# Two-layer decoder on one core: four engine blocks joined into one, with explicit waits at the stage borders

## The chip, the cores and the metric

The kernel runs on one core of a Trainium2 chip. The metric is the device time in microseconds (us) of the slowest core; with one core that is the time of the run. The engines of a core are PE (TensorE, matrix products), DVE (VectorE), ACT (ScalarE), POOL (GpSimd) and SP (SyncE, which here issues nearly all DMAs).

## The reference

The reference is a decoder of six steps, each added to the rows x (4 batches of 256 tokens, 256 wide) and followed by a layer norm:

```
x = _layernorm(x + _L0_attn_ref(x, ...))           # 16 heads of 128, causal, biases
x = _layernorm(x + _L0_xattn_ref(ctx_512, x, ...)) # top-76 graph of the context
x = _layernorm(x + _L0_ffn_ref(x, ...))            # 32 masked ternary experts, top-1
x = _layernorm(x + _L1_attn_ref(x, ...))           # 16 heads, 4 key heads, rotary
x = _layernorm(x + _L1_xattn_ref(x, ctx_512, ...)) # cross attention with a norm inside
x = _layernorm(x + _L1_ffn_ref(x, ...))            # 16 experts, top-4, and a shared one
```

Everything is float32; products are made as three products of high and low parts.

## The kernel before

The program has four stages, one after the other, each written as a function with a body for each of the five engines:

- `attention(c, 0, ...)`: the first attention, in 16 steps (`s`), one pair of heads for half the tokens each. Its last step ends with products into banks 0 and 1 on PE, and two additions of these banks to x on DVE (L1202, in `output`). DVE counts each bank that it has emptied on the semaphore `s_taken`; the two last additions are the last two counts. Meanwhile POOL multiplies the last expert masks with the ternary weights (L568, in `Masks.mask`), for the next stage.
- `graph_and_masked_experts`: DVE takes the moments of x (L1345, L1351), POOL makes the reciprocal root (L1372, L1376, in `Norm.root`), DVE scales; this twice. PE turns the masked expert weights (`turn`, L1610) and ACT copies them (L1682); then x is turned (`turned2`, L1409), the tokens are sorted by expert with indirect DMAs, multiplied, and stored in that order (`y_sorted`, L1564, on SP's queue). At the end POOL waits until all stores have landed and gathers the rows of the first half of the tokens with four indirect DMAs (`weights.gather`, L464). DVE adds and normalises them (`weights.sums`, L471, L473, L475; `norm3.apply`, L1392), PE turns them (`turned3.pe`, L1409), ACT copies the high parts to `xt_hi` (L1415) and DVE subtracts to get `xt_lo` (L1421). DVE's last act in this stage is the second of these subtractions.
- `attention(c, 1, ...)`: the second attention. SP first loads the weights q and k of head group 1 (into `spare`), then those of group 2 (into `raw_q`, `raw_k`, L490); PE's first products (L125 to L127) read `xt_hi` and `xt_lo`.
- `cross_and_experts`: DVE takes moments (L1345), POOL makes roots, DVE applies them (L1392), PE turns x (`turned4`) after 20 idle products that keep it running (`keep_warm`, L147); then cross attention and a loop over 20 pieces of experts.

Each engine runs its own list of instructions in order. What orders them against one another inside a stage is semaphores alone. Between stages stands the end of one `with nc.Block()` and the start of the next: there every engine, SP included, arrives at a meeting, and none goes on before all have arrived. The four blocks so have three meetings between them, from here on border 1 (first attention to graph), border 2 (experts to second attention) and border 3 (second attention to cross attention).

Of the kernel before, what the change touches and what calls it, by code (L numbers as in the profile page):

```python
# [11 lines left out]
P = 128  # L12
# [55 lines left out]
def decoder(nc, a, out):  # L68
    with ExitStack() as ctx:
# [43 lines left out]
        c.masks = Masks(c)  # L113
        with AttentionWeights(c, 0) as weights, Beginning(c) as beginning:
            attention(c, 0, weights, beginning)
# [289 lines left out]
class AttentionWeights:  # L405
# [12 lines left out]
    def __enter__(self):  # L418
# [12 lines left out]
        self.own = Count(S("pool"))  # L431
        if self.rope:
# [171 lines left out]
def attention(c, layer, weights, beginning=None):  # L604
# [19 lines left out]
    number = ring_units(units, rope)  # L624

# [23 lines left out]
    with ExitStack() as ctx:  # L649
# [21 lines left out]
        s_taken = S("taken")  # L671
# [26 lines left out]
        with nc.Block() as block:  # L698
            @block.sync
            def _(sp):  # L700
                if rope:
                    weights.load(sp, "q", 1)
                    weights.load(sp, "k", 1)
                else:
                    beginning.loads(sp, weights)
                for g in range(1, LAST_GROUP + 1):
                    if not rope or g < LAST_GROUP:
                        sp.wait_ge(s_split_proj, g * STEPS)
                        weights.load(sp, "q", g + rope)
                        weights.load(sp, "k", g + rope)  # L710
                    if not rope:
                        sp.wait_ge(s_split_v, g)
                        weights.load(sp, "v", g)
                    if not rope and g == LAST_GROUP:
                        for pair in range(4, 6):
                            c.masks.load(sp, pair)
                    sp.wait_ge(s_split_o, g)
                    weights.load(sp, "o", g)
                    if not rope and g >= 5:
                        for pair in ((0, 1), (2, 3), range(6, c.masks.PAIRS))[g - 5]:  # L720
                            c.masks.load(sp, pair)
                    if not rope and g == 2:
                        blank = c.idle[:].bitcast(F32).unsqueeze(1).broadcast_to([P, CHUNKS * BANK // P, D])
                        sp.dma_start(c.sorted_rows.rearrange("(t p) d -> p t d", p=P), blank).then_inc(c.s_blank, 16)

            @block.gpsimd
            def _(pool):
                def split_proj(s):

                    if s >= STEPS:  # L730
                        pool.wait_ge(s_proj, PROJ_BEFORE[s - STEPS + 1])
                    weights.split_proj(pool, s)

                def split_v(g):
                    if g:
                        pool.wait_ge(s_v, g * (NT // 2))
                    weights.split_all(pool, "v", g, s_split_v)

                def split_o(g):
                    if g:  # L740
                        pool.wait_ge(s_o, g * 2)
                    weights.split_all(pool, "o", g, s_split_o)

                def rotate(s):

                    for u, (what, j) in enumerate(units(s) if rope else ()):
                        n = PROJ_BEFORE[s] + u
                        dst = queries[:, j] if what == "q" else keys[:, group_of(s, what) % 2]
                        pool.wait_ge(s_taken, taken("proj", s, u))
                        nc.gpsimd.tensor_tensor(dst, along[:, n % 2], across[:, n % 2], ALU.add).then_inc(s_rope, 1)  # L750

                def ternary():

                    pool.wait_ge(c.s_ffn_weight, 16)
                    nc.gpsimd.tensor_scalar(c.clipped[:], c.ffn_weight[:], 2.0, 1.0, ALU.mult, ALU.min)
                    pool.drain()
                    nc.gpsimd.tensor_scalar(c.ffn_weight[:], c.clipped[:], -1.0, 12582912.0, ALU.max, ALU.add)
                    pool.drain()
                    nc.gpsimd.tensor_scalar(c.tern[:], c.ffn_weight[:], -12582912.0, None, ALU.add)
                    nc.gpsimd.memset(c.minus_two[:], -2.0)  # L760
                    pool.drain()
                    nc.gpsimd.tensor_tensor(c.less_sq[:], c.one_less[:], c.minus_two[:], ALU.pow)

                MASKED_AT = {10: (0, 1), 12: (2, 3), 13: (4, 5), 14: range(6, c.masks.AFTER_KEPT), LAST: range(c.masks.AFTER_KEPT, c.masks.PAIRS)}

                def masks(s):

                    for pair in MASKED_AT.get(s, ()):
                        if pair == c.masks.AFTER_KEPT:
                            pool.wait_ge(s_kept, 1)  # L770
                            pool.drain()
                        c.masks.mask(pool, pair)

                batches = lambda ap: ap[:].rearrange("p (b t) -> p b t", b=B)
                whole = c.one[:].broadcast_to([P, NTOK])
                values = c.kv[:].rearrange("p t n -> p (t n)")
                weighted = values
# [1397 lines left out]
```

## Time and profile before

| | us |
|---|---|
| median of 3 runs | 872.15 |
| lowest and highest of them | 869.73 and 873.27 |
| the profiled execution, its own time | 867.87 |
| its span, first to last instruction | 866.0 |

The profiled execution shows the busy time of each engine and, instruction by instruction, how long the engine was idle before it and what ended the idle time. In its rows the time in brackets is that idle time. A number at the start of a row is its start in us from the start of the span, the second is how long it took. "SPq" is a DMA being issued on SP; "PEq L698" as a releaser is an instruction of the queue itself, here the branch after a meeting.

### The profile page before, as it was taken

The numbers are of one execution on the slowest core, as the hardware profiler recorded it, in microseconds if no ns is written. First come the engines' busy times: TensorE is split into PE (matmuls) and PEld (weight loads), VectorE is DVE, ScalarE is ACT, GpSimd is POOL, SyncE is SP. The second block draws the span as 40 slices with busy tenths as digits, with TensorE's granted clock in tenths as the row PEclk, the third lists the DMA queues.
The fourth block names the chain that finished last, engine by engine and source line by source line (L and its number), as shares of the span: only waits on it lengthen the run. The fifth ranks groups of instructions, "written<-read, shape, count | busy, mean of one in ns | idle before, by whom it ended". The sixth has DMA issues, their size and how long they took to land. (4 is left out here: it accounts for less than half of the span.)

```text
span 866.0 us, 14628 instructions
## 1 busy us (share of the span) xinstructions
PE 789.9 (91%) x4731; PEld 677.8 (78%) x4737; DVE 572.2 (66%) x1661; ACT 421.5 (49%) x1193; POOL 498.8 (58%) x407
## 2 busy tenths in 40 slices
PE   8999999999999876694899989999986899999995
PEld 5878898888888864392788878898874588888884
DVE  5796876967768477223778877786737646455555
ACT  3473644636546545171475745766754532323232
POOL 6667369657587351612585546357512387776763
PEclk9999999999999988897999999999999899999998
DMA  8121620212315212553220111010001011111111
GB/s 226 57 97 34 211 70 30 98 64 84 132 37 175 73 55 68 189 115 82 62 79 6 51 55 56 1 56 26 25 1 38 13 55 36 55 36 55 45 35 48
DMA packets 58332, 59.09 MB, mean 68 GB/s; under 512 B 5392, under 2 KB 49312, under 8 KB 58272
## 3 DMA queue, kind: packets, MB, share of 16 engines
q1 hardware_dynamic: 57504, 56.24, 21.1%
q0 software_dynamic: 768, 2.10, 0.8%
q8 instruction: 32, 0.52, 0.2%
q14 instruction: 28, 0.23, 0.1%
HBM read 50.00 MB, written 8.32 MB: 67 GB/s over the span
## 5 line engine op out<-in xcount | busy, mean ns | idle before, releaser
L1049 ACT ACTIVATE a_probs<-bank,a_neg_peak 128x128 f32<-128x128 f32 (+1 forms) x256 | 103.2, 428 | 95.5 <-DVE a_neg_peak L1169 95.5
L1169 DVE CUSTOM_DVE_ANT_0 bank<-bank,causal 128x128 f32<-128x128 f32 (+1 forms) x256 | 82.6, 392 | 32.9 <-PE bank L902 32.9
L1077 ACT ACTIVATE a_probs<-a_probs,a_row_inv 128x128 f32<-128x128 f32 (+1 forms) x256 | 92.1, 454 | 9.5 <-DVE a_row_inv L1177 9.5
L1055 ACT ACTIVATE a_probs_t<-bank 128x512 f32<-128x512 f32 x96 | 54.1, 601 | 60.8 <-PE bank L922 60.8
L941 PE MATMUL bank<-a_probs_t,a_vals 128*128 128x256 f32 x256 | 77.9, 387 | 3.3 <-DVE a_ot_lo L1189 3.3
L1900 POOL TENSOR_TENSOR d_h_lo<-d_h,d_h_hi 128x512 fp32r<-128x512 f32 x40 | 51.7, 1293 | 45.6 <-ACT d_h_hi L2020 32.0
L125 PE MATMUL bank<-a_wo_hi,a_ot_hi 128*128 128x256 f32 x256 | 72.8, 284 | 4.3 <-issue 4.3
L750 POOL TENSOR_TENSOR a_queries<-sim 128x512 f32<-128x512 f32 x32 | 41.0, 1282 | 60.7 <-DVE sim L1144 60.7
L2106 DVE TENSOR_TENSOR d_h<-d_silu,bank 128x512 f32<-128x512 f32 x40 | 27.5, 688 | 71.8 <-PE bank L127 70.5
L127 PE MATMUL bank<-a_wo_hi,a_ot_lo 128*128 128x256 f32 x256 | 71.8, 280 | 0.0
L126 PE MATMUL bank<-a_wo_lo,a_ot_hi 128*128 128x256 f32 x256 | 71.7, 280 | 0.0
L2113 DVE SCALAR_TENSOR_TENSOR x<-bank,d_gate,x 128x256 f32<-128x256 f32 x160 | 64.5, 476 | 2.4 <-PE bank L127 0.2
L505 POOL TENSOR_TENSOR a_wk_hi<-raw_k,one 128x512 fp32r<-128x512 f32 (+1 forms) x20 | 19.2, 958 | 78.3 <-DMA raw_k<-in_L_attn_w_k_dram 75.6
L125 PE MATMUL bank<-xt_hi,d_w_hi 128*128 128x512 f32 x160 | 63.5, 397 | 0.0
L126 PE MATMUL bank<-xt_lo,d_w_hi 128*128 128x512 f32 x160 | 63.2, 395 | 0.0
L127 PE MATMUL bank<-xt_hi,d_w_lo 128*128 128x512 f32 x160 | 63.2, 395 | 0.0
L908 PE MATMUL bank<-a_keys,a_queries 128*128 128x256 f32 x256 | 60.6, 379 | 0.0
L147 PE MATMUL bank<-idle 128*128 128x512 bf16 x98 | 32.7, 504 | 29.6 <-DMA sim<-y_sorted,a_place 9.9
L922 PE MATMUL bank<-ident,a_probs 128*128 128x128 f32 x384 | 53.2, 274 | 4.8 <-ACT a_probs_t L1055 4.6
L922 PEld LDWEIGHTS bank<-ident,a_probs 128*128 128x128 f32 x384 | 45.3, 140 | 14.7 <-ACT a_probs_t L1055 6.5
L1144 DVE TENSOR_TENSOR sim<-bank,a_sin 64x512 f32<-64x512 f32 x80 | 55.1, 688 | 1.1
L1049 ACT ACTIVATION_READ_ACCUMULATOR a_probs<-bank,a_neg_peak 128x1 f32 x256 | 55.1, 215 | 0.0
(328 smaller groups left out, 2408.8 us busy)
## 6 DMA issues: line engine op xcount, KB each, us to landing
d_raw<-in_L_ffn_we_dram SPq DMA_DIRECT2D x48, 128.0 KB, 2.2
raw_k<-in_L_attn_w_k_dram SPq DMA_DIRECT2D x8, 512.0 KB, 6.9
raw_q<-in_L_attn_w_q_dram SPq DMA_DIRECT2D x8, 512.0 KB, 6.3
raw_v<-in_L_attn_w_v_dram SPq DMA_DIRECT2D x8, 512.0 KB, 7.5
raw_o<-in_L_attn_w_o_dram SPq DMA_DIRECT2D x8, 512.0 KB, 3.7
kv<-_L_ffn_expert_masks_dram SPq DMA_DIRECT2D x16, 256.0 KB, 2.9
kvt<-_L_ffn_expert_masks_dram SPq DMA_DIRECT2D x16, 256.0 KB, 3.1
raw_o<-in_L_attn_Wo_dram SPq DMA_DIRECT2D x8, 512.0 KB, 3.6
```

The source lines that it names most:

```text
L125: nc.tensor.matmul(out, l_hi, r_hi, start=start, stop=False)
L126: nc.tensor.matmul(out, l_hi, r_lo, start=False, stop=False)
L127: return nc.tensor.matmul(out, l_lo, r_hi, start=False, stop=stop)
L908: last = nc.tensor.matmul(out, queries[:, j, row + P:row + T], keys_of(s, j)[:, row:row + width], start=True, stop=True)
L922: last = nc.tensor.transpose(c.banks[3 + turned % 2][:, slot % 4 * P:(slot % 4 + 1) * P], probs[s % 2][:, i, at:at + P], c.ident[:])
L941: nc.tensor.matmul(out, vals_of(s)[:, 2 * i, cols], probs_t[:, at:at + T], start=True, stop=False)
L1049: nc.scalar.activation(probs[s % 2][:, i, at:at + width], c.banks[i][:, at:at + width], ACT.Exp, bias=neg_peak[:, n:n + 1], scale=-1.0, ac ...
L1055: nc.scalar.activation(probs_t[:, i * BANK:(i + 1) * BANK], c.banks[3 + (3 * s + i) % 2][:], ACT.Copy).then_inc(s_pt_free, 1)
L1077: last = nc.scalar.activation(part, part, ACT.Copy, scale=row_inv[:, s % 2, n + r:n + r + 1])
L1144: last = nc.vector.tensor_tensor(two(across[to:to + HALF_BLOCK, n % 2]), two(bank[at:at + HALF_BLOCK]), many(sin[at:at + HALF_BLOCK], HALF ...
L1169: last = nc.vector.tensor_tensor_reduce(part, part, mask, -1.0, 3e38, ALU.add, ALU.min, neg_peak[:, n + r:n + r + 1])
L2113: last = nc.vector.scalar_tensor_tensor(c.x[:, t], c.banks[4 + u][:, (t % 2) * D:(t % 2 + 1) * D], g, c.x[:, t], ALU.mult, ALU.add, accum_ ...
```

## The change

One block is opened in `decoder` and all four stages write their bodies into it, so the three meetings go. `s_taken` moves to the object that outlives the stage, and `c.s_added`, `c.added` are this semaphore and its final count, which stands for "both last additions to x are done". Four lines of waits stand in place of the meetings: SP and PE wait for `c.added` at border 1, PE waits for the low parts of the turned rows at the end of the expert stage (border 2), SP waits for `c.added` at border 3. Of the diff, what is only indented differently is left out:

```
@@ decoder
+        c.block = ctx.enter_context(nc.Block())
         with AttentionWeights(c, 0) as weights, Beginning(c) as beginning:
             attention(c, 0, weights, beginning)
@@ AttentionWeights.__enter__
+        self.s_taken = S("taken")
@@ attention
     number = ring_units(units, rope)
+    c.s_added, c.added = weights.s_taken, len(number) + 2
...
-        s_taken = S("taken")
+        s_taken = weights.s_taken
...
-        with nc.Block() as block:
+        block = c.block
@@ graph_and_masked_experts
-        with nc.Block() as block:
+        block = c.block
...
+            sp.wait_ge(c.s_added, c.added)
             for sem in c.finished:
                 sp.sem_clear(sem)
...
+            pe.wait_ge(c.s_added, c.added)
             for pair in range(0, 11):
                 turn(pair)
...
                 turned3.pe(pe, s_norm3, 4, range(1))
                 keep_warm(c, 6)
+            turned3.wait(pe, 0)
@@ cross_and_experts
-        with nc.Block() as block:
+        block = c.block
             @block.sync
             def _(sp):
+            sp.wait_ge(c.s_added, c.added)
                 sp.dma_start(wr[:], a["L1_ffn_w_router"]...)
```

What stands on DVE at border 1, before the change: the last additions to x, two branches of which the second waits for the meeting, and the first moments of the graph stage.

```order
575 L1243 TENSOR_TENSOR sim<-sim,bank 128x512 [waits a0_kept_t] x4
576 L1202 TENSOR_TENSOR x<-x,bank 128x512 [waits a0_o] x2
577 L698 UNCONDITIONAL_BRANCH
578 L1718 UNCONDITIONAL_BRANCH [waits barrier_Pool_Activation_PE_DVE_SP_release]
579 L1345 BN_STATS b_b_norm_stats<-x 128x6 x4
580 L1351 BN_AGGR b_b_norm_mv<-b_b_norm_stats 128x2 x4
```

The same place on DVE after the change:

```order
575 L1246 TENSOR_TENSOR sim<-sim,bank 128x512 [waits a0_kept_t] x4
576 L1205 TENSOR_TENSOR x<-x,bank 128x512 [waits a0_o] x2
577 L1724 UNCONDITIONAL_BRANCH
578 L1348 BN_STATS b_b_norm_stats<-x 128x6 x4
579 L1354 BN_AGGR b_b_norm_mv<-b_b_norm_stats 128x2 x4
```

One branch and the wait are gone; the moments follow the additions. No other instruction of DVE moved, here or elsewhere.

What stands on SP at border 2, before the change: the last stores of the experts' rows, the load of the output weights, the meeting, and the loads of the second attention.

```order
108 L1564 DMA y_sorted<-kvt 64x4x256 [waits b_y]
109 L1564 DMA y_sorted<-kv 64x3x256 [waits b_y]
110 L490 DMA raw_o<-in_L_attn_Wo_dram 128x4x256 [waits b_stored1]
111 L1556 UNCONDITIONAL_BRANCH
112 L699 UNCONDITIONAL_BRANCH [waits barrier_Pool_Activation_PE_DVE_SP_release]
113 L490 DMA spare<-in_L_attn_Wq_dram 128x2x512
114 L490 DMA spare<-in_L_attn_Wk_dram 128x2x128
115 L490 DMA raw_q<-in_L_attn_Wq_dram 128x2x512 [waits a1_split_proj]
116 L490 DMA raw_k<-in_L_attn_Wk_dram 128x2x128
117 L490 DMA raw_o<-in_L_attn_Wo_dram 128x4x256 [waits a1_split_o]
```

The same place on SP after the change:

```order
109 L1567 DMA y_sorted<-kv 64x3x256 [waits b_y]
110 L492 DMA raw_o<-in_L_attn_Wo_dram 128x4x256 [waits b_stored1]
111 L702 UNCONDITIONAL_BRANCH
112 L492 DMA spare<-in_L_attn_Wq_dram 128x2x512
113 L492 DMA spare<-in_L_attn_Wk_dram 128x2x128
114 L492 DMA raw_q<-in_L_attn_Wq_dram 128x2x512 [waits a1_split_proj]
115 L492 DMA raw_k<-in_L_attn_Wk_dram 128x2x128
116 L492 DMA raw_o<-in_L_attn_Wo_dram 128x4x256 [waits a1_split_o]
```

Nothing stands any longer between the load of the output weights and the four loads behind it: two wait for nothing, and two for the splits of group 0 (`a1_split_proj`), which POOL makes in the middle of the expert stage. Only the load in row 116 waits for something of the second attention.

## Rows read from the trace of the kernel before

**Rows 1.** Windows by stage: busy time of each engine, clock, DMA share, GB/s.

```profile
core 0: us, PE busy (x) PEld busy (x) DVE busy (x) ACT busy (x) POOL busy (x), PEclk, DMA share, GB/s
0.00:317.10 317.10, 304.94 (x1768) 263.73 (x1770) 231.40 (x724) 161.12 (x500) 203.36 (x133) 1.00 0.30 98
317.10:410.60 93.50, 65.99 (x474) 50.31 (x476) 41.13 (x116) 39.70 (x61) 29.71 (x30) 0.84 0.39 107
```

**Rows 2.** Timeline at border 1, all engines.

```profile
313.50 1.28 DVE L1202 TENSOR_TENSOR x<-x,bank 128x512 f32<-128x512 f32 x2
313.52 0.28 PE L127 MATMUL bank<-a_wo_hi,a_ot_lo 128*128 128x256 f32 x1
314.65 2.12 POOL L568 TENSOR_TENSOR raw_q<-kvt,tern 128x1024 bf16<-128x1024 f32 x1 [0.19 <-DMA kvt<-_L_ffn_expert_masks_dram]
317.11 1.41 DVE L1345 BATCH_NORM_STATS2 b_b_norm_stats<-x 128x6 f32<-128x256 f32 x4 [2.33 <-PEq L698]
317.12 1.86 PE L1610 MATMUL bank<-ident_bf,spare 128*128 128x128 bf16 x16 [3.31 <-PEq L698]
319.08 0.27 POOL L1372 TENSOR_SCALAR b_b_norm_shifted<-b_b_norm_mv,less_sq 128x4 f32<-128x4 f32 x1 [2.32 <-DVE b_b_norm_mv L1351]
```

**Rows 3.** Timeline where PE first waits for x in the graph stage.

```profile
329.31 1.09 PE L1409 MATMUL bank<-ident,x 128*128 128x128 f32 x8 [1.27 <-DVE x L1732]
```

**Rows 4.** Timeline at border 2: DVE, SP, ACT, PE.

```profile
409.06 1.29 DVE L1421 TENSOR_TENSOR xt_lo<-bank,xt_hi 128x512 fp32r<-128x512 f32 x2 [1.38 <-ACT xt_hi L1415]
410.63 0.38 SPq L490 DMA_DIRECT2D spare<-in_L_attn_Wq_dram  x1
410.67 0.47 PE L125 MATMUL bank<-xt_hi,a_wk_hi 128*128 128x512 f32 x1 [0.55 <-PEq L1556]
```

**Rows 5.** Timeline at border 3: DVE, PE.

```profile
648.39 1.40 DVE L1202 TENSOR_TENSOR x<-x,bank 128x512 f32<-128x512 f32 x2 [1.19 <-PE bank L127]
648.78 0.28 PE L127 MATMUL bank<-a_wo_hi,a_ot_lo 128*128 128x256 f32 x1
650.28 1.46 DVE L1345 BATCH_NORM_STATS2 d_d_norm_stats<-x 128x6 f32<-128x256 f32 x4 [0.50 <-PEq L698]
650.62 4.26 PE L147 MATMUL bank<-idle 128*128 128x512 bf16 x19 [1.56 <-PEq L698]
655.47 1.09 PE L1409 MATMUL bank<-ident,x 128*128 128x128 f32 x8 [0.59 <-DVE x L1392]
```

**Rows 6.** Timeline of a hand-over from DVE to PE inside a stage.

```profile
682.14 1.29 DVE L1421 TENSOR_TENSOR xt_lo<-bank,xt_hi 128x512 fp32r<-128x512 f32 x2 [0.18 <-ACT xt_hi L1415]
683.48 0.50 PE L1451 MATMUL bank<-xt_hi,d_wr_split 128*128 128x512 f32 x1 [0.21 <-DVE xt_lo L1421]
```

**Rows 7.** Timeline before border 2: last store, load, first gather, fourth gather, DVE.

```profile
392.80 0.60 SPq L490 DMA_DIRECT2D raw_o<-in_L_attn_Wo_dram  x1
395.88 1.01 POOL L464 DMA_INDIRECT sim<-y_sorted,a_place  x1 [6.81 <-DMA y_sorted<-kv]
398.69 0.43 DVE L471 TENSOR_TENSOR sim<-sim,rows 128x256 f32<-128x256 f32 x1 [12.50 <-DMA sim<-y_sorted,a_place]
399.70 0.94 POOL L464 DMA_INDIRECT sim<-y_sorted,a_place  x1 [0.30 <-issue]
402.88 0.41 DVE L471 TENSOR_TENSOR sim<-sim,rows 128x256 f32<-128x256 f32 x1
```

**Rows 8.** Windows around the gathers, and of the four loads (columns as above).

```profile
392.50:396.50 4.00, 0.00 (x0) 0.00 (x0) 0.00 (x0) 0.00 (x0) 0.62 (x1) 0.82 0.95 229
396.50:397.50 1.00, 0.00 (x0) 0.00 (x0) 0.00 (x0) 0.00 (x0) 0.69 (x2) 0.50 0.03 8
412.50:416.50 4.00, 4.00 (x19) 3.23 (x18) 3.92 (x6) 0.00 (x0) 1.29 (x1) 1.00 1.00 281
```

**Rows 9.** DMA issues between 384 and 412: KB each, us to landing.

```profile
spare<-in_L_attn_Wq_dram SPq DMA_DIRECT2D x1, 512.0 KB, 5.6
sim<-y_sorted,a_place POOLq DMA_INDIRECT x4, 2.7
```

**Rows 10.** DMA packets between 420 and 440, when only the second half's gathers run.

```profile
DMA packets 193, 0.53 MB, mean 27 GB/s; under 512 B 64, under 2 KB 64, under 8 KB 192
```

**Rows 11.** Windows at and after border 1, and a later one (columns as above).

```profile
317.10:322.00 4.90, 4.24 (x37) 3.64 (x38) 4.74 (x20) 3.56 (x4) 2.32 (x4) 0.50 0.11 27
327.00:332.00 5.00, 2.74 (x27) 2.24 (x25) 4.75 (x23) 3.43 (x6) 1.39 (x2) 1.00 0.01 2
```

**Rows 12.** DMA issues of the whole program: the router weights of the last stage.

```profile
d_wr<-in_L_ffn_w_router_dram SPq DMA_DIRECT2D x1, 16.0 KB, 1.8
```

More of the change, by code:

```diff
@@ L670, in attention @@
         s_proj, s_v, s_pv, s_o = S("proj"), S("v"), S("pv"), S("o")
-        s_taken = S("taken")
+        s_taken = weights.s_taken
         s_ot_hi = S("ot_hi")
@@ new lines, in output @@
+            def output(g):
+                pe.wait_ge(s_split_o, g + 1)
+                pe.wait_ge(s_taken, taken("pv", g * STEPS + 1, 1))
+                for u in range(2):
+                    bank = claim("o", g, u)
+                    for i in range(2):
+                        cols = slice((2 * u + i) * P, (2 * u + i + 1) * P)
+                        for h in range(GROUP):
+                            last = mm3(nc, bank[:, i * D:(i + 1) * D], ot_hi[:, h, cols], ot_lo[:, h, cols], weights.hi["o"][:, h], weights.lo["o"][:, h],
+                                       h == 0, h == GROUP - 1)
+                    last.then_inc(s_o, 1)
@@ new lines, in _ @@
+            for s in range(LAST + 1):
+                late = rope and s % STEPS
+                count = len(units(s + 2)) if s + 2 <= LAST else 0
+                early = max(count - 1, 0)
+                if s < LAST:
+                    scores(s + 1)
+                else:
+                    last_output(range(0, 2))
+                if not late:
+                    proj(s + 2, range(0, early))
+                first = 1 if rope and count else 2
+                transposes(s, range(0, first))
+                proj(s + 2, range(0, min(count, 1)) if late else range(early, count))
+                transposes(s, range(first, 3))
+                pv(s)
+                if late:
+                    proj(s + 2, range(1, count))
+                if rope and s == PASS_STEPS - 2:
+                    values(1)
+                if s % STEPS and s < LAST:
+                    if not rope:
+                        values(s // STEPS + 1)
+                    output(s // STEPS)
+                if rope and s == TURN_STEP:
+                    turn()
@@ new lines, in _ @@
+        @block.gpsimd
+        def _(pool):
+            norm1.roots(pool, c.less_sq[:])
+            norm2.roots(pool)
+            pool.wait_ge(c.s_blank, 16)
+            pool.wait_ge(s_place, 1)
+            for t in range(NT):
+                nc.gpsimd.indirect_dma_start(c.sorted_rows, bass.IndirectOffsetOnAxis(place[:, t:t + 1], 0), c.x[:, t], None).then_inc(s_scattered, 16)
+            pool.wait_ge(s_turned, PAIRS)
+            weights.first_splits(pool)
+            pool.wait_ge(s_xt, XT + CHUNKS * KC)
+            weights.second_splits(pool)
+            for i in range(STAGES):
+                pool.wait_ge(s_stored[i], 16 * 2 * CHUNKS // STAGES)
+            weights.gather(pool, 0)
+            weights.root(pool, 0)
```

1998 lines of the change are left out of this document (977 added, 1021 removed).

## The prediction

> **What bounds the kernel now.** I read first the windows by stage. Up to border 1 PE is busy 304.94 of 317.10 us; in the stage from border 1 to border 2 it is busy 65.99 of 93.50 us [rows 1]. So in the attentions PE is the bound, while the graph and expert stage is a chain from engine to engine and DMA. What stands at a border is on the path in any case, because every engine has to go through it. Then I read the timeline at each border, for two numbers: when does the work end on which the next stage depends, and when does the next stage begin. The gap between them is all that a meeting can cost.
>
> **Border 1.** DVE's second addition to x ends at 313.50 + 1.28 = 314.78. DVE takes its first moments at 317.11, after 2.33 us idle. The engine that came last to the meeting is POOL: its last mask ends at 314.65 + 2.12 = 316.77, and 0.34 us later the others go on [rows 2]. The masks are not needed for the moments. That the moments are the path is seen later: PE, having turned eleven pairs of weights, waits 1.27 us for the normalised x [rows 3].
>
> With the meeting gone, DVE's list goes from the additions straight to the moments. Half 0 is ready for POOL 319.08 - 317.11 = 1.97 us after DVE starts, so at about 314.78 + 1.97 = 316.75. POOL ends its mask at 316.77: it is free just as it is asked, and behind the mask only this root stands in its list. So POOL's tail doesn't eat the gain. A branch remains on DVE. The gain has 2.33 us as its upper end and, should POOL's root still start only 0.34 us after the mask, 319.08 - 317.11 = 1.97 as its lower; I take 2.2. PE waits for the same additions by the new wait and starts its turns by about the same amount earlier; it has 1.27 us of cover before it is asked, and would cost its excess only if it came more than that later than DVE's chain. SP's clears and the load of the numbers shift along, since SP waits for the same count.
>
> The clock changes here too, but off the path. After the idle 3.31 us [rows 2] PE has 0.50 of its clock in the next 4.9 us, the lower level of 1.2 GHz; in a window with a gap of 1.27 us before a product [rows 3] the granted clock is 1.00, 2.4 GHz [rows 11]. Without the meeting PE's gap is from 313.80 to about 314.9, some 1.1 us, so it may stay at the upper level. The turns then end sooner, and PE waits longer for x. This is worth nothing as long as DVE's chain is the later one.
>
> **Border 2.** DVE's last subtraction ends at 409.06 + 1.29 = 410.35 and PE's first product begins at 410.67, a gap of 0.32 us [rows 4]. PE now waits for just this subtraction, and a branch stands between. A hand-over from DVE to PE within a stage takes 683.48 - 683.43 = 0.05 us [rows 6]. So the gap shrinks to between 0.05 and 0.32; with the branch I take 0.15, a gain of 0.17. ACT's scaling of the cosines is not asked for until PE's first products are done, and costs or gives nothing.
>
> **Border 3.** DVE's last addition ends at 648.39 + 1.40 = 649.79, the moments begin at 650.28: 0.50 us idle, with DVE itself the last to arrive [rows 5]. It now runs on after a branch. The gain is between 0 and 0.50; I take 0.4, as nothing but the branch is left. PE's 20 idle products start about 1.4 us earlier, as PE ended at 649.06 and began them at 650.62. They then end near 653.4, while x is there at about 655.47 - 0.4 = 655.1. PE's gap before turning x grows from 0.59 to 1.6 us. Gaps of 1.27 us left the clock at 1.00 [rows 3, 11] and one of 3.31 brought 0.50 [rows 2, 11], so 1.6 is nearer to the harmless one. SP's loads start 0.3 us earlier and are hidden.
>
> The three gains make 2.2 + 0.17 + 0.4 = 2.8 us, at most 2.33 + 0.27 + 0.50 = 3.1, at least 1.97.
>
> **What the change adds.** The meeting at border 2 also held SP. SP issues the output weights at 392.80 and the next four loads only from 410.63 on [rows 4, 7]. Without the meeting they follow at once, from about 393.4: two loads of 512 KB and two of 128 KB, 1.31 MB. They wait for nothing that is not done by then. Their start earlier gives nothing: at 410.63 they were already hidden behind other work of the second attention.
>
> But they now run beside the four gathers. POOL issues the first gather at 395.88, and DVE, idle for 12.50 us, starts on its rows at 398.69; from there to the last tile it works without a gap, some 1.4 us a tile (402.88 - 398.69 over three) [rows 7]. So the first gather's landing is on the path one to one. The later ones are issued every 1.27 us and have a little slack, the fourth lands at 399.70 + 2.7 = 402.4 for a use at 402.88 [rows 7, 9].
>
> In the profile the DMA engines are full (0.95) until 396.5 with the last store and the output weights and nearly empty (0.03) from there to 397.5, just before the first gather's data move [rows 8]. After the change the gap is filled: the same 1.31 MB at the 281 GB/s that these loads reached [rows 8] are 4.7 us, from 396.5 to about 401.2, over the first three gathers.
>
> What this costs the first gather no row shows, since no gather of this kernel ran beside a load. The lower bound is 0, if the engines have room. The upper bound is that the gather waits until all 1.31 MB are through: its data would move at 401.2 instead of 397.5, 3.7 us late, less what the later gathers catch up, nothing. Between them: the records of the gathers are 192 packets for four, of which 64 are under 512 B, so 32 data packets of 4 KB and 16 small ones a gather [rows 10], or two large ones and one small on each of 16 DMA engines. If each of the three waits for one 2 KB packet of a load, at 281/16 = 17.6 GB/s that is 3 x 0.12 = 0.35 us. I take 0.5 us, nearer the low end, since the load's packets are small beside the gather's own.
>
> The page "DMA: Bandwidth & Descriptors" of the Trainium skill (Queues, rings and completion order) speaks against this: a DMA engine serves its queues in turn but changes only after a packet of some 9 to 17 descriptors, and a completion count lands only after the earlier writes of its engine. No run here shows it yet; it is weighed as a rival.
>
> **The sum.** 2.8 - 0.5 = 2.3 us. Against the profiled execution's own 867.87 us that is 865.6 us. The profiled one was 0.5% faster than the median of the runs shown, so the same 2.3 us from 872.15 give 869.85 us. That is 0.26%, less than the 0.5% that a measurement of this kernel can tell from no change.
>
> **The rivals.**
> - *A load's whole share goes ahead of a gather.* One 512 KB load holds the engines for 512 KB at 281 GB/s, 1.9 us, before the first gather is served. For it speaks that loads and gathers are on different queues of the same 16 engines; against it that each 2 KB is a packet of its own in the records. Sum: 2.8 - 1.9 = 0.9, 871.2 us. This is what the page's rule would do, 16 rows of 2 KB on each engine being within its 9 to 17.
> - *The gathers wait for all loads.* 3.7 us against 2.8: 873.0 us, slightly slower. It needs one order for both queues.
> - *A branch that waits for code.* Slower than before, at the borders: the one branch left leads to code that isn't there yet. In the profile both branches and the meeting fit into 0.32 to 0.50 us [rows 4, 5], which speaks against it, but the single block may lay the bodies out differently. The nearest price is the landing of a 16 KB load, 1.8 us [rows 12]. At one border it takes 1.8 of the 2.3 us, 871.6 us; from two on the kernel is slower; at all three 5.4 - 2.3 = 3.1 us, 875.2 us. The page "Runtime: NRT & Kernel Launch" (Instruction fetch mechanics) says that a taken branch out of the fetched window forces such a load.
> - *More than the sum.* The higher clock after border 1 and engines that run ahead save on the path what I have counted as cover. For over 0.5% this must bring 2 us on top of the 2.3, 867.8 us or less. Nothing in the rows names it, apart from PE's low clock after the gap.
>
> **Chances and range.** My forecast 0.53, a whole share ahead 0.18, all loads ahead 0.09, a branch that waits 0.08, more than the sum 0.12. Low end: all gains at their upper ends and no delay give 869.0, and the runs of before lie up to 2.4 us under their median, so 866.8. High end: the gathers behind all loads, 873.0, and a little scatter, 873.4; this leaves out part of the two outer rivals and of the scatter, some 2 in 10. Faster by over 0.5% (under 867.8) comes from the rival that brings more and the low scatter, 0.13; slower by over 0.5% (above 876.5) from the branches alone with scatter, 0.06; the rest is 0.81.
>
> **What would show it.** Border 1: DVE's moments within 0.2 us of the addition's end, POOL's root within 0.1 us of its mask's end, the graph stage's rows 2.2 us earlier up to the gathers. Border 2: SP's four loads issued between 393 and 396 in the old time, the DMA engines full past 397.5, and the gather's time from issue to landing above 2.7; PE's first product 0.15 us after DVE's subtraction. Border 3: moments right behind the additions, PE's gap before L1409 near 1.6 us and the clock still 1.00 after it. I am wrong if the gather takes 4 us or more to land, if a gap of over 1 us remains at a border, or if POOL's root turns out late.

## The result, and the profile after

The changed kernel takes 875.35 us, median of 13 runs (873.20 to 878.44). The kernel before, on the same chip and in turn with it, takes 872.15 us, median of 13 (868.20 to 874.18). The ratio is 1.0041 with a 95% interval of 1.0025 to 1.0057. The change costs 3.6 us where I forecast a gain of 2.3.

The profiled execution of the changed kernel took 878.44 us with a span of 876.8; that of before took 867.87 with 866.0. These differ by 10.6 us, the medians by 3.2. Both profiled executions lie at an outer end of their kernel's runs. So the two traces have to be read stage by stage, and each difference held against the profiles of further runs, before any of it is put down to the change.

First the windows by stage; to be read against [rows 1]. The third window is the one that [rows 11] shows for before, the fourth the place where x is turned, the last that of the gathers.

```profile
core 0: us, PE busy (x) PEld busy (x) DVE busy (x) ACT busy (x) POOL busy (x), PEclk, DMA share, GB/s
0.00:317.06 317.06, 305.48 (x1768) 263.61 (x1769) 233.70 (x724) 161.41 (x500) 201.47 (x133) 1.00 0.31 98
317.06:419.07 102.01, 68.70 (x475) 52.94 (x477) 41.51 (x117) 40.69 (x63) 31.49 (x31) 0.80 0.39 111
317.10:322.00 4.90, 3.11 (x45) 2.54 (x46) 4.75 (x21) 4.14 (x5) 4.34 (x5) 1.00 0.09 27
329.30:334.00 4.70, 4.05 (x30) 3.65 (x31) 4.16 (x17) 2.43 (x5) 0.08 (x1) 0.64 0.01 2
400.00:406.00 6.00, 0.00 (x0) 0.00 (x0) 0.00 (x0) 0.00 (x0) 3.87 (x4) 0.50 0.99 341
```

The first attention ends at the same time as before although the meeting behind it is gone: this one execution lost 2.3 us inside it, which other runs of the same kernel didn't (last section). The graph stage is 8.5 us longer. Nearly half of that is not the change: 3.9 us lie between the experts' first maximum and the first gather, where PE waits 3.13 us for a load of sorted rows instead of 1.84 and then turns them at half the clock. The second profile of the same kernel has 1.1 us more there than before, and one profile of the kernel with the drains (below) has 3.5. While the four gathers run, the DMA engines are full (0.99) with 341 GB/s, where before they had a share of 0.34 in the 7 us from the first gather's issue on.

**Border 1**, timeline, against [rows 2, 3]:

```profile
315.87 1.28 DVE L1205 TENSOR_TENSOR x<-x,bank 128x512 f32<-128x512 f32 x2
316.93 2.13 POOL L570 TENSOR_TENSOR raw_q<-kvt,tern 128x1024 bf16<-128x1024 f32 x1
317.06 1.40 DVE L1348 BATCH_NORM_STATS2 b_b_norm_stats<-x 128x6 f32<-128x256 f32 x4
317.20 1.07 PE L1614 MATMUL bank<-ident_bf,spare 128*128 128x128 bf16 x16 [1.03 <-DVE x L1205]
319.16 0.27 POOL L1375 TENSOR_SCALAR b_b_norm_shifted<-b_b_norm_mv,less_sq 128x4 f32<-128x4 f32 x1
329.36 1.20 PE L1412 MATMUL bank<-ident,x 128*128 128x128 f32 x8 [2.40 <-DVE x L1738]
331.14 1.97 PE L1412 MATMUL bank<-ident,x 128*128 128x128 f32 x8 [0.59 <-DVE x L1738]
```

The two additions end at 315.87 + 1.28 = 317.15 and the moments are recorded from 317.06, 0.08 us before that: nothing stands between them any more, against 2.33 us. PE waits 1.03 us instead of 3.31 and keeps 1.00 of its clock. It reaches the place where x is turned early and waits 2.40 us there instead of 1.27. Eight turns take 1.97 us where the eight before them took 1.20: the granted clock fell to half there, and it did not in the first profile of the kernel before. It would be easy to put this down to the longer wait. But the second profile of the kernel before, with its meeting and the same wait of 1.27 us, has all sixteen turns at half the clock:

```profile
333.64 3.75 PE L1409 MATMUL bank<-ident,x 128*128 128x128 f32 x16 [1.27 <-DVE x L1732]
```

So the low clock at the turns of x is not new, and the length of the wait alone does not decide it.

**Border 2**, timeline, against [rows 4, 7]. SPq rows are the issues of loads.

```profile
397.35 0.60 SPq L492 DMA_DIRECT2D raw_o<-in_L_attn_Wo_dram  x1
398.00 0.65 SPq L492 DMA_DIRECT2D spare<-in_L_attn_Wq_dram  x1
398.70 0.48 SPq L492 DMA_DIRECT2D spare<-in_L_attn_Wk_dram  x1
399.23 0.47 SPq L492 DMA_DIRECT2D raw_q<-in_L_attn_Wq_dram  x1
399.74 0.47 SPq L492 DMA_DIRECT2D raw_k<-in_L_attn_Wk_dram  x1
400.54 1.01 POOL L466 DMA_INDIRECT sim<-y_sorted,a_place  x1 [6.93 <-DMA y_sorted<-kv]
406.30 0.42 DVE L473 TENSOR_TENSOR sim<-sim,rows 128x256 f32<-128x256 f32 x1 [15.56 <-DMA sim<-y_sorted,a_place]
417.85 0.69 DVE L1424 TENSOR_TENSOR xt_lo<-bank,xt_hi 128x512 fp32r<-128x512 f32 x1 [0.16 <-ACT xt_hi L1418]
419.07 0.58 PE L126 MATMUL bank<-xt_hi,a_wk_hi 128*128 128x512 f32 x1
```

The four loads that stood behind the meeting now follow the output weights at once and are all issued before the first gather. From the gather's issue to DVE's first rows it takes 406.30 - 400.54 = 5.76 us; before it was 398.69 - 395.88 = 2.81. The subtraction ends at 418.54 and PE begins 0.53 us later, against 0.32.

**Border 3**, timeline, against [rows 5]:

```profile
658.36 1.40 DVE L1205 TENSOR_TENSOR x<-x,bank 128x512 f32<-128x512 f32 x2 [1.19 <-PE bank L128]
659.67 1.40 DVE L1348 BATCH_NORM_STATS2 d_d_norm_stats<-x 128x6 f32<-128x256 f32 x4
661.89 0.20 POOL L1375 TENSOR_SCALAR d_d_norm_shifted<-d_d_norm_mv 128x4 f32<-128x4 f32 x1 [18.65 <-DVE d_d_norm_mv L1354]
663.57 1.02 POOL L1379 TENSOR_TENSOR d_d_norm_rstd<-d_d_norm_shifted,half_neg 128x4 f32<-128x4 f32 x1 [1.48 <-issue]
666.07 1.09 PE L1412 MATMUL bank<-ident,x 128*128 128x128 f32 x8 [2.71 <-DVE x L1395]
```

DVE's gap of 0.50 us is gone. But from its moments to PE's turns it is now 666.07 - 659.67 = 6.40 us, where it was 655.47 - 650.28 = 5.19. The new time stands in POOL: 1.48 us of idle time between its first and second instruction, with "issue" as releaser. Between the two stands `pool.drain()` (L1378, in `Norm.root`), an instruction that ends when the work ahead of it is done. The timeline leaves drains out, but the trace's instruction records have them: this one takes 1.63 us and ends 1.38 us behind POOL's first instruction, where the same drain of the kernel before (L1375) takes 0.31 us and ends 0.06 behind it. The records of the instruction queue q14 also have a block of 8 KB that moves from 662.57 to 663.03, in this gap; in the kernel before it came at 651.3, ahead of POOL's first instruction. When I planned the runs below I took this block for POOL's code and the gap for the wait for it. The records of q14 name no engine, and the runs speak against it, as is said behind them.

PE's gap before it turns x is 2.71 us, and the eight turns behind it take 1.09 us, the full clock.

### The profile page after: what moved, and what is told of

It is laid out like the page before. It is cut to its first block, busy times and chain, and to the rows that moved or that the text cites. A ratio compares the mean times of both kernels' runs of the same rounds, so it can differ in the third digit from the quotient of the medians.

```text
span 876.8 us, 14597 instructions
## 1 busy us (share of the span) xinstructions
PE 794.8 (91%) x4731; PEld 681.4 (78%) x4737; DVE 575.1 (66%) x1661; ACT 422.4 (48%) x1193; POOL 499.1 (57%) x407
## 3 DMA queue, kind: packets, MB, share of 16 engines
q1 hardware_dynamic: 57504, 56.24, 20.8%
## 4 chain that ended last, share of the span: by engine, by line
PE 63%; DVE 15%; issue 7%; POOL 5%; DMA 3%; DVEq 3%; ACT 2%; POOLq 1%; SPq 0%
PE bank L126 14%; PE bank L128 14%; PE bank L127 14%; PE bank L911 4%; PE bank L944 4%; PE bank L905 3%; DVEq L1219 2%; PE bank L925 2%; DVE bank L1172 2%; DVE a_top L1221 2%; PE bank L945 2%; POOL a_queries L753 2%; DVE a_work L1223 1%; PE bank L1650 1%; PE bank L1651 1%
## 5 line engine op out<-in xcount | busy, mean ns | idle before, releaser
L148 PE MATMUL bank<-idle 128*128 128x512 bf16 x98 | 34.3, 522 | 29.7 <-DMA sim<-y_sorted,a_place 11.1
```

## The experiments

All ratios are to the kernel before, run in turn on the same chip. The stage times stand in the table behind the experiments.

**The changed kernel again.**

> The changed kernel once more, for a second profile and as the reference of the other three. Loads theory (the four weight loads that SP now issues at the end of the expert stage hold back the first gather): about 1.004 of the kernel before, and the first gather again reaches VectorE 5 to 6 us after its issue, where it was 2.8. Clock theory (the lower TensorE clock now falls on waited-for products in the graph stage): 1.004 as well, with the stretches at half clock near 330, 358 to 371, 399 to 419 and 440 us again, and the kernel before free of those at 330, 368 and 440. Chance theory (the profile's lag of 2.3 us already at the end of the first attention is no part of the change): two copies of 2 us on VectorE near 119 and 227 us are gone or elsewhere in this profile.

Measured: 1.0054 [1.0031, 1.0077], median 876.09. The span of its profile is 872.5, 4.3 us less than that of the first. The gather's delay (5.93 us), the low clock where x is turned and the 6.40 us at border 3 come again; the 2.3 us lost in the first attention do not. So the last one belongs to that execution. The delay and the 6.40 us belong to the change; of the low clock this can't be said, since the kernel before shows it too.

**The four loads held back until the gathers have landed**, all else as changed:

```
+            if rope:
+                for t in HALF_TILES[0]:
+                    sp.wait_ge(weights.s_got[t], 16)
                 weights.load(sp, "q", 1)
```

> The changed kernel with one more wait on SP: the four loads of the second attention are issued only when the four gathers of the first half have landed. Loads theory: the first gather's rows reach VectorE 2.8 us after its issue, and the time falls by 2.9 us against the changed kernel, to 0.9965 of it, about 1.000 to 1.001 of the kernel before. Clock theory: the gather gets faster, but at least half of the loss stays, 1.002 to 1.003 of the kernel before or more. If the three border gains are real and nothing else is lost, it comes out at 0.997.

Measured: 1.0012 [0.9994, 1.0030]. Its timeline:

```profile
397.31 1.01 POOL L466 DMA_INDIRECT sim<-y_sorted,a_place  x1 [6.82 <-DMA y_sorted<-kv]
400.15 0.42 DVE L473 TENSOR_TENSOR sim<-sim,rows 128x256 f32<-128x256 f32 x1 [12.55 <-DMA sim<-y_sorted,a_place]
403.95 0.38 SPq L492 DMA_DIRECT2D spare<-in_L_attn_Wq_dram  x1
```

The gather is back at 2.84 us, and 0.42% of the 0.54% are gone, some 3.7 us. The second attention, which uses these loads, takes 240.4 us, between the 239.1 and 240.9 of the two profiles of the kernel before: no gain of the loads' early start can be seen.

**The kernel before with its meetings, and only the four loads early:**

```
 in the graph stage's list of SP, behind weights.load(sp, "o", 0)
+    weights.load(sp, "q", 1)
+    weights.load(sp, "k", 1)
+    sp.wait_ge(weights.s_split_proj, STEPS)
+    weights.load(sp, "q", 2)
+    weights.load(sp, "k", 2)
```

The attention's own list loses these four loads and the wait between them.

> The kernel before, all three meetings in place, with only these four loads moved ahead of the meeting at border 2. Loads theory: 2.9 us slower than the kernel before, 1.003 to 1.004. Clock theory: within 0.001 of the kernel before.

Measured: 1.0064 [1.0042, 1.0087], more than expected. Its timeline has the gather's delay with every meeting in place:

```profile
394.41 0.65 SPq L490 DMA_DIRECT2D spare<-in_L_attn_Wq_dram  x1
396.95 1.01 POOL L464 DMA_INDIRECT sim<-y_sorted,a_place  x1 [6.94 <-DMA y_sorted<-kv]
402.58 0.42 DVE L471 TENSOR_TENSOR sim<-sim,rows 128x256 f32<-128x256 f32 x1 [15.46 <-DMA sim<-y_sorted,a_place]
```

402.58 - 396.95 = 5.63 us. Together with the held loads this shows the cause from both sides: it is enough to move the loads, and enough to move them back. In this profile the hand-over at border 2 took 1.06 us instead of 0.32 as well, of which the cause isn't known; with it the gather (+2.8), the turns behind it (+0.7) and the hand-over (+0.7) make some +4.3 us, within the interval's 3.7 to 7.6.

**Only border 1 joined** (the first block closed behind the graph stage, the second attention and the last stage each in a block of their own), run twice:

```
+        first = ExitStack()
+        c.block = first.enter_context(nc.Block())
...
+            first.close()
+            with nc.Block() as c.block:
+                attention(c, 1, weights)
+        with nc.Block() as c.block:
+            cross_and_experts(c)
```

> Only the meeting at border 1 is taken out, those at borders 2 and 3 stay, so the four loads are issued where they were. Sum of the prediction: 2.2 to 2.4 us faster than before, 0.9973. Clock theory: the products of the graph stage run partly at half clock where they did not before, and the gain is lost, 1.000 or more.

> Border 1 alone joined, once more, to narrow its interval: 0.9987 before. If the 2.4 us at the border arrive in full it is 0.9972; with about 1 us given back to the lower clock in the graph stage, 0.9984. In the profile the gap before the moments is gone and the stretch from the turned x to the logits' maximum is at least 0.3 us longer than the 12.2 + 8.6 us of the kernel before.

Measured: 0.9987 [0.9971, 1.0003] and 0.9987 [0.9972, 1.0001]. The gap at border 1 closes by the full 2.4 us, but the kernel gains 1.1, between the 0.9973 of the sum and the 1.000 of the clock theory; both intervals just reach the former, at 0.9971 and 0.9972, and just take in 1.000. The stage times have a part of the rest: from the moments to the experts' first maximum the joined kernels take 22.0 us in the mean of ten profiles (21.2 to 23.3), those with a meeting 21.1 in the mean of three (20.8 to 21.3).

**The kernel before again**, to see how far profiles of one kernel lie apart:

> The kernel before against itself: 1.000. Its second profile tells chance from change in two stretches in which the first profile was faster than all later ones, the second attention (239.1 us against 240.3 to 240.7) and the way from the sort's result to the first turned chunk (17.2 against 17.5). Chance: this profile shows 240.5 and 17.5 too. Change: it shows 239.1 and 17.2 again.

Measured: 0.9997 [0.9974, 1.0019], but a span of 872.9 against 866.0. The first attention and the second each differ from one profile to the next by some 2 us and more, with stretches at half the clock that come and go. The second attention takes 240.9 us here, so the 239.1 of the first profile was chance.

**Held loads, and the meeting at border 3 back:**

> The kernel with held loads, but with the meeting at border 3 back in place; borders 1 and 2 stay joined. Code theory (without the meeting GpSimd fetches a piece of its code between its first and second instruction of the last stage, 1.3 us on the path, where it fetched it before them while it was idle): from the moments to the first turned x 5.2 us instead of 6.4, the gap before the moments 0.50 us again, 0.6 us faster than with held loads alone. Other theory (the 1.3 us come from the engines' changed timing at border 2): 6.4 us stay.

Measured: 0.9984 [0.9964, 1.0003]. From the moments to the turns it takes 5.48 us, with the 0.50 us of the meeting ahead of it again. POOL's second instruction follows the first at once, 655.73 and 655.87.

**Held loads, all joined, and eight drains of POOL behind its work in the second attention.** They were meant to do nothing but move POOL's later instructions on by eight places:

```
+            if rope:
+                for _ in range(8):
+                    pool.drain()
```

> Held loads, all three borders joined, and eight drains added on GpSimd at the end of the second attention, where it has been idle for long. They only push its later instructions back in its code. Code theory: the fetch falls before the first root's wait and is hidden; 5.2 us from the moments to the first turned x with no gap ahead of the moments, 1.2 us faster than with held loads alone, in all about 0.9985 to 0.9975 of the kernel before. If the stall belongs to the branch or to the power function and not to the place in the code, 6.4 us stay.

> Held loads and eight drains, all borders joined, once more to narrow its interval: 0.998 of the kernel before, that is 1.5 to 2 us faster; the first root's second instruction on GpSimd follows within 0.2 us of its first again. If it comes out at 1.000 or above, the code theory explains a stretch of the profile but no time.

Measured: 0.9981 [0.9962, 1.0000] and 0.9978 [0.9962, 0.9993], medians 870.65 and 869.28. Timeline at border 3 of the first:

```profile
652.86 1.40 DVE L1353 BATCH_NORM_STATS2 d_d_norm_stats<-x 128x6 f32<-128x256 f32 x4
655.08 0.20 POOL L1380 TENSOR_SCALAR d_d_norm_shifted<-d_d_norm_mv 128x4 f32<-128x4 f32 x1 [18.65 <-DVE d_d_norm_mv L1359]
655.43 1.02 POOL L1384 TENSOR_TENSOR d_d_norm_rstd<-d_d_norm_shifted,half_neg 128x4 f32<-128x4 f32 x1
658.26 0.99 PE L1417 MATMUL bank<-ident,x 128*128 128x128 f32 x7 [1.71 <-DVE x L1400]
```

POOL's second instruction follows 655.43 - 655.28 = 0.15 us behind the first, against 1.48, and the turns begin 5.40 us behind the moments, against 6.40. This kernel has the lowest ratios of the study, and the second run lies under the kernel before with its whole interval; it can't be told from the kernels with border 1 alone or with the meeting at border 3 back. The stage times make -1.5 us of it (with 0.9 us given back behind border 1), the runs -1.7 and -1.9.

**What the stall is.** The edit doesn't only move instructions: like the meetings, it puts a drain where there was none. The records of POOL's drains in all fourteen profiles are these, "beyond" being the time from the end of the work ahead to the end of the drain:

```
indirect DMAs since     beyond        which drain
the drain before
none                    0.05 to 0.07  all others that have work ahead of them
4                       0.41          meeting at border 3, where border 2 has a meeting too (5 profiles)
12                      1.07          meeting at border 2 (the same 5)
16                      1.40          meeting at border 3, where border 2 has none (1 profile)
16                      1.40          the first of the eight added drains (3 profiles)
16                      1.38          the drain in the first root of the last stage (the other 5)
```

That is some 0.085 us for each indirect DMA that POOL issued since its last drain, an estimate from these rows: (1.07 - 0.05)/12, (0.41 - 0.05)/4 and (1.38 - 0.05)/16. In the kernel before the meetings took this time while POOL was idle. Without them it falls on the first drain that is left, and in the changed kernel this is the one between the two instructions of the root, for which x waits. The eight drains and the meeting at border 3 pay the same 1.40 us between 635 and 638 us, some 18 us before anyone asks for POOL. The theory of the code has the records against it: in the first run with drains no block comes on q14 between 599.4 and 656.07, and that one moves behind POOL's second instruction, without a stall. Not run, and the direct test of this: one single drain behind the gathers.

**The same, with PE's turns at border 1 made to wait until the rows' roots are there,** which should bring the low clock back to where nobody waits and take it out of the turning of x:

```
+            pe.wait_ge(norm1.s_rstd, 1)
```

> As the last, and TensorE waits at border 1 until GpSimd has made the first root, so that it is again idle for over 3 us there. Clock theory: its clock is at the lower level right after border 1, where nobody waits for it, and at the higher one when it turns x for the experts' sort; from the turning of x to the logits' maximum 8.6 us as in the kernel before, instead of 9.3 to 10.9, so 0.5 to 1 us faster than the last. If the clock there is chance, no difference.

Measured: 0.9983 [0.9961, 1.0005]. Timeline at border 1 and at the turns of x:

```profile
318.64 1.51 PE L1619 MATMUL bank<-ident_bf,spare 128*128 128x128 bf16 x16 [4.63 <-issue]
328.67 1.92 PE L1417 MATMUL bank<-ident,x 128*128 128x128 f32 x16
```

The stretch at half clock stands at 319.1 to 322.5, and sixteen turns now take 1.92 us, the full clock (0.12 us each, as against 1.97 for eight). But PE came to them 1.4 us late, behind its weights, and over the whole stretch it took 21.67 us against 22.0: nothing that the time can show. That PE at full clock would save the 0.9 us is thus only argued from rows.

**How the queues share the DMA engines: half of the loads held** (only the second pair waits for the gathers):

```
                 if not rope or g < LAST_GROUP:
                     sp.wait_ge(s_split_proj, g * STEPS)
+                    if rope and g == 1:
+                        for t in HALF_TILES[0]:
+                            sp.wait_ge(weights.s_got[t], 16)
```

> The changed kernel, with only the second pair of the four loads (group 2, 640 KB) held until the gathers have landed; the first pair (640 KB) is still issued early. Queue theory (a gather's data move only when what the load queue had before it is nearly through): the load queue runs dry 1.9 us earlier, so the first gather's rows reach VectorE 3.0 to 3.9 us after its issue, between 2.8 and 5.8, and the time is 2 to 2.5 us less than the changed kernel's, 1.001 to 1.003 of the kernel before. Share theory (one whole 512 KB load goes ahead, whatever stands behind it): 4.6 us or more, since such a load is still there.

Measured: 1.0012 [0.9999, 1.0026].

```profile
395.26 0.67 SPq L492 DMA_DIRECT2D spare<-in_L_attn_Wq_dram  x1
397.77 1.01 POOL L466 DMA_INDIRECT sim<-y_sorted,a_place  x1 [6.89 <-DMA y_sorted<-kv]
401.24 0.43 DVE L473 TENSOR_TENSOR sim<-sim,rows 128x256 f32<-128x256 f32 x1 [13.24 <-DMA sim<-y_sorted,a_place]
```

401.24 - 397.77 = 3.47 us: with 640 KB ahead the delay is 0.7 us, with 1.31 MB 3.0. A delay of a fixed share would be equal in both. It grows with what the SP queue still holds when the gather is issued: from 1.7 us behind the issue, when an undisturbed gather's first row moves, to the first row that did move, SP's queue moved 145 KB here and 744 KB in the changed kernel.

**The loads held until the first gather has landed:**

> The changed kernel, with the four loads held only until the first gather has landed. Queue theory: the later gathers stand in their queue before the loads do and go through; from the first rows on VectorE to the turned x 9.05 us as ever. If loads overtake gathers that were issued before them, the fourth gather is late and this stretch is 0.5 us or more longer.

One execution, 872.33 us.

```profile
397.58 0.95 POOL L466 DMA_INDIRECT sim<-y_sorted,a_place  x1 [0.30 <-issue]
397.87 0.38 SPq L492 DMA_DIRECT2D spare<-in_L_attn_Wq_dram  x1
398.83 0.94 POOL L466 DMA_INDIRECT sim<-y_sorted,a_place  x1 [0.30 <-issue]
403.06 0.42 DVE L473 TENSOR_TENSOR sim<-sim,rows 128x256 f32<-128x256 f32 x1 [2.29 <-DMA sim<-y_sorted,a_place]
405.07 0.43 DVE L473 TENSOR_TENSOR sim<-sim,rows 128x256 f32<-128x256 f32 x1 [0.53 <-DMA sim<-y_sorted,a_place]
```

Here my picture of a single line by time of issue fell. The third gather is issued 0.3 us ahead of the first load, and DVE still has its rows only 5.5 us later; those of the fourth, issued among the loads, 6.2 us. This does not show that a load overtakes a gather that is ready: a load's first row moves 1.0 us behind its issue, here at 398.90, a gather's 1.7, which would have been 399.3. In the packets' records the third gather's rows begin at 400.78 and the fourth's at 402.60. From 400.78 to 404.30 both queues move, POOL's 252 KB and SP's 854 KB: beside a full SP queue the gathers get under a quarter, not nothing.

Stage times of the profiles, worked out from their timelines (us; "held" is the second experiment, "fill" the one with the eight drains, "border 1" the two with only that one joined; two numbers are two profiles):

```
                                     before        changed       loads early  held    border 1      fill
additions' end to moments            2.33, 2.17    -0.08,-0.08   2.24         -0.08   -0.08,-0.08   -0.08,-0.08
moments to the experts' maximum      20.80, 21.15  21.57, 21.93  21.29        23.28   21.16, 22.29  22.37, 22.26
that maximum to the first gather     58.0, 58.4    61.9, 59.1    58.6         57.8    57.9, 58.1    61.5, 58.1
first gather's issue to its rows     2.81, 2.77    5.76, 5.93    5.63         2.84    2.86, 2.81    2.87, 2.82
turn of x to xt_lo's end             2.61, 2.61    3.19, 3.32    3.30         2.61    2.61, 2.61    2.61, 2.61
xt_lo's end to PE (border 2)         0.32, 0.32    0.53, 0.28    1.06         0.29    0.57, 0.57    0.28, 0.28
second attention                     239.1, 240.9  240.7, 240.3  240.4        240.4   240.6, 238.9  238.9, 239.0
border 3, additions' end to moments  0.49, 0.50    -0.09,-0.09   0.50         -0.08   0.51, 0.49    -0.09,-0.09
border 3, moments to turns of x      5.19, 5.18    6.40, 6.40    5.18         6.40    5.12, 5.12    5.40, 5.40
last product to the end              9.8, 9.8      10.0, 10.0    9.9          10.1    9.9, 9.9      10.2, 10.1
```

## Why the prediction was wrong, point by point

**The step that failed is the price of the first gather beside the loads.** The prediction put it at 0.5 us, "nearer the low end, since the load's packets are small beside the gather's own". It measured 5.76 - 2.81 = 2.95 us, in what follows 3.0, and holding the loads back took all of it away again. The rows that should have made me careful were at hand: the loads were seen to use all of the DMA engines [rows 8], so there was no free room that a gather could have had. I worked with a turn for a turn between the queues, for which no row stood. In the packets' records of the changed kernel 1.11 of the 1.31 MB of loads move before the first row of the gather (1.16 and 1.13 MB in the two other profiles with all four loads early), 3.8 us behind its issue, where before it moved after 1.7. The rival of all loads ahead, priced at 3.7 us with 0.09, came nearest.

The Trainium skill, page "DMA: Bandwidth & Descriptors" (Queues, rings and completion order), has an engine change its queue after a packet of some 9 to 17 descriptors. That points in the right direction, and I gave it 0.18 at 1.9 us. In the three profiles some 36 packets of SP's queue on each engine went first in the time in which the gather's rows could have moved, an estimate that takes 1.7 us behind the issue for its start. The measurement decides: that is more than the rule gives. Why, the runs leave open. It could be a rank of the queues, or packets of a load that are longer than the records show. The loads from ACT's queue, or cut in smaller ones, weren't tried.

**Behind the gather, 0.65 us more.** PE's last turns in the graph stage, and what depends on them, took 3.2 to 3.3 us where they took 2.61, in each of the three profiles with all four loads early and in no other. The granted clock was 0.50 in them. The prediction had no term for this. PE's longer wait for the rows (11.1 us against 9.5 with the loads held) does not explain it alone: where the loads were held until the first gather had landed it waited 12.3 us, and the turns took 2.61.

**Border 1 was right in its size** (2.2 forecast, 2.4 measured; POOL's root starts 319.16 against its mask's end at 319.06, 0.10 us behind it) **and wrong in what follows.** The prediction said that the clock "changes here too, but off the path", and priced it at nothing. In the profiles the clock is low right behind the border, where PE has cover, in all three with a meeting there and in one of the ten without. It is low at the turns of x, where DVE and ACT wait for each turn, in all ten without the meeting and in two of the three with it. The first profile of the kernel before, from which I predicted, happens to be the third (1.00 in [rows 11], against 0.64 in 4.7 us of the changed kernel). The stretch up to the experts' maximum is longer by 0.9 us in the mean of the ten, and I put this against the 2.4. That it comes from the clock is only argued: single profiles of one kernel scatter by as much. My reading that a gap of 1.27 us leaves the clock at 1.00 was chance: behind the same 1.27 us the second profile has 0.50, and at border 3 a gap of 2.71 us has 1.00 behind it.

**Border 2** gains next to nothing: PE begins 0.28 or 0.29 us behind the subtraction in eight of the nine profiles without this meeting and 0.53 in one, against 0.32 in both of the kernel before; forecast was 0.15. With a meeting it took 0.57 in both profiles with border 1 alone joined and 1.06 in the one with early loads, so the scatter is wider than the gain.

**Border 3 was wrong in its sign.** "Nothing but the branch is left" holds for DVE, whose 0.58 us came. But the two meetings also paid for POOL's drains, 1.07 and 0.41 us, while it stood idle. Without them the 16 indirect DMAs are paid for in the drain of the first root, on the path: +1.2 us, net +0.6. The prediction had no term for this. The rival of a branch that waits for code comes near in size (1.8 forecast, 1.3 measured for the stall), but by luck: it is no branch, it isn't on DVE or PE, and the records of the drains speak against a wait for code.

**The end** of the program is 0.2 to 0.3 us longer. I don't know why.

**The sum** by what was measured: -2.4 + 0.9 + 3.0 + 0.65 + 0 + 0.6 + 0.2 = +3.0 us. The two ratios of the changed kernel give +3.6 and +4.7, with intervals of 1.4 and 2.0 us to each side. Two sums fit less well: with the loads held the stages make -0.7 us and the ratio says +1.0, just outside its interval of 1.6, and with half of them held 0 and +1.0. The profiles of these two have some 2.6 us more than the others in the last stage, and the one with PE's turns held at border 1 has 1.4; the profiles of the changed kernel and of the two fill runs have none of it. How often their other executions have it isn't known, so this stays open as the missing term.

## What to carry to other kernels

A meeting of all engines also holds back the transfers of the engine that issues them. Before it is taken away, ask what the freed queue will issue into, and whether a transfer that is waited for runs at that time; if so, hold the loads by a wait for it, which cost nothing that could be seen in the stage that uses them. A meeting also drains POOL: behind indirect DMAs keep a drain at a place where POOL is idle, before the first one that someone waits for. Where a stall is removed from PE, look for the wait that grows in its place and what is done right behind it, and read the clock there in more than one profile before putting it down to the change. Two profiles of one kernel differed here by 7 us; a stage time is worth believing when it comes again in a second one.

## What the hardware showed unexpectedly

- A gather through POOL's queue gets little of the DMA engines while SP's queue has rows: 2.8 us to its rows with an empty queue, 3.5 with 640 KB ahead, 5.6 to 5.9 with 1.31 MB, and 5.5 to 6.2 when the loads were issued about when it was. With both queues at work POOL's moved 252 KB while SP's moved 854.
- A drain of POOL takes longer by some 0.085 us for each indirect DMA that was issued since the drain before: 0.41 us beyond the work ahead of it with 4, 1.07 with 12, 1.38 to 1.40 with 16, and 0.05 to 0.07 with none.
- A copy of 128 x 256 on DVE took far longer where it started just after a POOL operation. The next two rows are of the first attention, the first of the changed kernel's timeline and the second of the kernel before's:

```profile
118.69 2.00 DVE L1216 COPY a_work<-sim 128x256 f32<-128x256 f32 x1
```

```profile
118.62 0.75 DVE L1213 COPY a_work<-sim 128x256 f32<-128x256 f32 x1
```

  In the changed kernel a POOL operation of 1.90 us had begun at 118.64, 0.05 us ahead of the copy, and the copy ends 0.15 us behind it, after 2.00 us; the same came again at 226.63 (1.92 us against 0.49), 0.12 us behind the start of a POOL operation of 1.89 us. Copies of this shape take 0.28 us at the least. The two copies, 1.25 and 1.43 us longer, make up what the first attention lost in that one execution. The Trainium skill, page "SBUF — State Buffer" (Who interferes with whom), gives the two engines one shared pair of ports that the first to start holds to its end; the rows agree.
- Stretches at half the clock add up to 51 us within one profile of the kernel before and to 68 in another. The second attention, from PE's first product to the end of the additions, takes 240.3 to 240.9 us in the ten profiles that have such a stretch between 428 and 440 us and 238.9 to 239.1 in the four that have none, with or without the change.
